# Gate and up products in a ring of three PSUM banks, and layer norms applied by ScalarE

## The chip, the cores and the metric

The kernel runs on one core of one Trainium2 chip. The metric is device time in microseconds (us) of one execution. The engines are TensorE (PE; its weight loads are PEld), VectorE (DVE), ScalarE (ACT), GpSimd (POOL) and SyncE (SP), which issues DMAs. Each runs its own instructions in program order and waits on semaphores.

## The reference

For x and a context of 16 sequences x 64 positions x 256 channels (1024 tokens), and 32 experts of width 96:

```
x = x + wkv(w, u, layernorm(x), ctx)         # keys from the norm, values from ctx
x = x + experts(layernorm(x))
layernorm(x) = (x - mean) / sqrt(var + 1e-5)
wkv, per channel, over positions t:  y = (A p + E v) / (A q + E), with decaying sums p, q
experts: softmax(x @ gate_w), the best 8 of 32, weights made to sum to 1,
  at most 64 x 8 = 512 tokens an expert (in order of tokens), then
  y = (silu(x @ w_gate[e]) * (x @ w_up[e])) @ w_down[e], weighted and summed over e
```

## The kernel before, in words

All tensors are fp32. A product of two fp32 matrices is done as three TensorE products: each operand is split into a rounded high part (made by ScalarE: whi, t_hi, h_hi, tile_hi) and the rest (wlo and t_lo by GpSimd, h_lo and tile_lo by VectorE).

**Tokens.** 1024 tokens are eight tiles of 128. The experts are computed for the first four tiles (half 0), then for the last four (half 1), for every expert with the routing weight, which is zero where an expert wasn't chosen. The first four tiles are made ready in the part before the first turn, as two units of two tiles. The other four tiles are single-tile units (slot 2): the early one partly before the first turn, the others one by one beside the expert work of half 0.

**Turns and steps.** A group is four experts, whose 384 hidden channels are three steps of 128. A turn is two groups, so six steps (k = 0 to 5); four turns (0 to 3) make a half, 24 steps. A step n on TensorE is, in order: the up product of n (six matmuls of 512 columns, `project` with part 1), when k is 0 or 3 the routing weights spread over the channels (`weights`), then small work beside it, the gate product of n+1 (`project`, part 0, six matmuls), and the down product of n-1 (`down`, six matmuls). On ScalarE a step is silu of the gate product into s_sb (L476), t_hi (L481), and a third of the next group's weights rounded, whi (L455). On VectorE: t1 = weights x silu (L977) and t = t1 x up product (L983). On GpSimd: t_lo (L348) and wlo (L323). s_sb, t1_sb and t_sb are single; t_hi, t_lo and the weights have two buffers.

**PSUM.** The gate product has two banks, 2 and 6, by the parity of k (`g_ps`), the up product one, bank 3 (`u_ps`). So the gate product of n waits for silu of n-2 (s_ready, L625) and the up product of n for t of n-1 (t_ready, L622).

**Beside half 0.** In each turn but the last a front unit (a tile) goes through its first norm at k = 0 (`stats_x`, `norm_x`), transposes and keys (`turn_kv` at k = 1, L550, `exps` at k = 2), recurrence (`recur`, at k = 3), mix and second norm (k = 4 and 5: `mix`, `turn_mixed` L559, `add_mixed`, `norm_h`); the unit before it, back, is transposed (`turn_h`, L572), split, and routed: `logits` (k = 1), `choose` (2), `ranks` (3), `weigh` (4), `turn_parts` (5, L614) and `take_route`. The lists `beside` in VectorE's and ScalarE's `turn` set after which step each stands. In turn 0 the early unit's second norm comes first.

**A norm.** VectorE makes mean and variance (`norm_stats`, L795 to L802, into mv and var), GpSimd var^-0.5 (`power`, L330), and VectorE (x - mean) x rstd, tile by tile (`norm_apply`, L807). TensorE transposes the normed tile; that is what releases `turn_kv` and `turn_h`. `keep_clock` are matmuls of zeros that fill waits before the first turn.

Of the kernel before, what the change touches and what calls it, by code (L numbers as in the profile page):

```python
# [8 lines left out]
ALU = mybir.AluOpType  # L9
# [3 lines left out]
P = 128  # L13
# [47 lines left out]
def program(nc, x, ctx_in, decay, bonus, gate_w, w_gate, w_up, w_down, out):  # L61
# [13 lines left out]
    GT = EG * INTER // P  # L75
# [14 lines left out]
    with ExitStack() as stack:  # L90
# [42 lines left out]
        var, rstd = sets("var", lambda n: [P, n]), sets("rstd", lambda n: [P, n])  # L133
        normed = sets("normed", lambda n: [P, n, C])
# [30 lines left out]
        y_ps, g_ps, u_ps, w_ps = bank[0:2], (bank[2], bank[6]), bank[3], bank[4]  # L165


# [128 lines left out]
        def _(pool):  # L296
# [67 lines left out]
            with pool.Fori(0, TURNS - 1) as it:  # L364
                turn(0, it, later(it + 3), later(it + 2))
            turn(0, TURNS - 1, None, later(TURNS + 1))
# [6 lines left out]
        def _(act):  # L373
# [22 lines left out]
            def exps(u):  # L396

                act.wait_ge(k_turned if u.slot < 2 else v_turned, u.n + 1)
                per, cols = u.tiles * BPT, u.tiles * P
                for k in range(KT):  # L400
                    fr = k_ps[u.slot][:, k * cols:(k + 1) * cols].rearrange("p (b s) -> p b s", s=S)
                    last = nc.scalar.activation(keys[u.slot][:, k * per:(k + 1) * per, 1:], fr, ACT.Exp,
                                                bias=shift[:, k:k + 1])
                last.then_inc(keys_ready, 1)

# [53 lines left out]
            for u in first_units:  # L459
                exps(u)  # L460
            act.wait_ge(gate_landed, 16)
# [6 lines left out]
            for u in first_units:  # L468
                take_h(u)
            route_exps(first_routed)  # L470

            def step(n, k, between=None):
# [3 lines left out]
                nc.scalar.activation(s_sb[:], g_ps[k % 2][:], ACT.Silu).then_inc(s_ready, 1)  # L476
# [6 lines left out]
            def turn(half, it, front, back, routed, first_turn=False, final=False):  # L483
# [45 lines left out]
        def _(pe):  # L529
# [87 lines left out]
            def project(n, half, part, slot, j, odd, group):  # L617
# [63 lines left out]
            def turn(half, it, front, back, routed, first_turn=False, last_turn=False):  # L681

                for k in range(TURN_STEPS):
                    n = it * TURN_STEPS + (half * STEPS + k)
                    slot, j = k // GT, k % GT
                    if half or not first_turn or k:
                        project(n, half, 1, slot, j, k % 2, it * 2 + (half * GROUPS + slot))
                    if back and first_turn and k == 1:

                        project(n + 1, half, 0, 0, 2, 0, 0)  # L690
# [24 lines left out]
                    elif k < TURN_STEPS - 1 or not last_turn:  # L715
                        project(n + 1, half, 0, (k + 1) // GT % 2, (k + 1) % GT, (k + 1) % 2,
                                it * 2 + (half * GROUPS + (k + 1) // GT))
                    elif half == 0:

                        pe.wait_ge(h_lo_kept, LATER)  # L720
                        project(n + 1, 1, 0, 0, 0, 0, GROUPS)
# [27 lines left out]
            project(0, 0, 0, 0, 0, 0, 0)  # L749
            project(0, 0, 1, 0, 0, 0, 0)  # L750
            ranks(first_routed)
            project(1, 0, 0, 0, 1, 1, 0)
# [16 lines left out]
        def _(dve):  # L769
# [22 lines left out]
            def norm_stats(src, *units):  # L792
# [11 lines left out]
            def norm_apply(u, src, ready, norm):  # L804
                dve.wait_ge(rstd_ready, norm + 1)
                for t in range(u.tiles):
                    last = nc.vector.tensor_scalar(normed[u.slot][:, t, :], src[:, u.tile + t, :], mv[u.slot][:, t, 0:1],  # L807
                                                   rstd[u.slot][:, t:t + 1], ALU.subtract, ALU.mult)
                last.then_inc(ready, 1)
# [4 lines left out]

            def norm_x(u):
                norm_apply(u, x_sb, k_normed, u.first_norm)
# [67 lines left out]
            def norm_h(u):  # L884
                norm_apply(u, x1, h_normed, u.second_norm)

# [63 lines left out]
            for u in first_units:  # L950
                norm_x(u)
            stats_x(early)
            recur(first_units[0])
            norm_x(early)
# [5 lines left out]
            for u in first_units:  # L960
                norm_h(u)
# [10 lines left out]
            def step(n, group):  # L972
# [10 lines left out]
                nc.vector.tensor_tensor(t_sb[:], u_ps[:], t1_sb[:], ALU.mult).then_inc(t_ready, 1)  # L983

            def turn(half, it, front, back, routed, first_turn=False):
                beside = {0: [(stats_x, front), (h_low, back), (norm_x, front)],
                          1: [(largest, routed)], 2: [(choose, routed)], 3: [(recur_and_invert, front)],
                          4: [(mix, front), (weigh, routed)], 5: [(add_mixed, front), (norm_h, front)]}
                if first_turn:
                    beside[0] = [(add_mixed, early), (norm_h, early)] + beside[0]  # L990
                for k in range(TURN_STEPS):
                    step(it * TURN_STEPS + (half * STEPS + k), it * 2 + (half * GROUPS + k // GT))
# [68 lines left out]
```

## Time and profile before

| what | value |
|---|---|
| median of 3 runs | 302.23 us (300.11 to 303.28) |
| the profiled execution: time / span | 300.93 us / 299.5 us |
| busy of the span: PE, PEld | 85%, 65% |
| busy of the span: DVE, ACT, POOL | 57%, 45%, 56% |
| granted clock of TensorE, mean | 0.924 |
| chain that ended last, by engine | PE 58%, DVE 24%, issue 11%, DMA 2%, POOL 2%, ACT 1% |

The part before the first turn ends at about 49.2 us, half 0 at about 195 us, half 1 at 294 us. A busy share is an average over these parts; a row of the table of stretches gives it for one. In a timeline row the bracket at the end is the time the engine stood idle before the instruction, and what released it. TensorE's granted clock is a share of its full 2.4 GHz; 0.50 is 1.2 GHz.

### The profile page before, as it was taken

The numbers are of one execution on the slowest core, as the hardware profiler recorded it, in microseconds if no ns is written. First come the engines' busy times: TensorE is split into PE (matmuls) and PEld (weight loads), VectorE is DVE, ScalarE is ACT, GpSimd is POOL, SyncE is SP. The second block draws the span as 40 slices with busy tenths as digits, with TensorE's granted clock in tenths as the row PEclk, the third lists the DMA queues.
The fourth block names the chain that finished last, engine by engine and source line by source line (L and its number), as shares of the span: only waits on it lengthen the run. The fifth ranks groups of instructions, "written<-read, shape, count | busy, mean of one in ns | idle before, by whom it ended". The sixth has DMA issues, their size and how long they took to land.

```text
span 299.5 us, 3887 instructions
## 1 busy us (share of the span) xinstructions
PE 255.4 (85%) x1077; PEld 194.1 (65%) x1077; DVE 169.9 (57%) x341; ACT 134.5 (45%) x211; POOL 168.3 (56%) x128
## 2 busy tenths in 40 slices
PE   5253889599399985999769997999999999999993
PEld 1222376487277764777548875787877878778772
DVE  5899956838965399544996438231533233223333
ACT  3442033293325833267334764254535635454421
POOL 5090100666445664466546776385878678786730
PEclk9956889989879995799979998899999999999999
DMA  6926000006005060140502314413250605430002
GB/s 200 291 76 158 0 2 0 0 1 165 14 0 158 0 175 2 27 131 0 158 0 64 94 46 114 102 57 87 73 146 12 160 12 146 101 126 0 0 2 71
DMA packets 39326, 22.23 MB, mean 74 GB/s; under 512 B 34192, under 2 KB 37264, under 8 KB 39312
## 3 DMA queue, kind: packets, MB, share of 16 engines
q1 hardware_dynamic: 38464, 21.63, 26.6%
q10 hardware_dynamic: 848, 0.43, 0.6%
q8 instruction: 7, 0.11, 0.2%
q14 instruction: 7, 0.06, 0.1%
HBM read 21.01 MB, written 1.05 MB: 74 GB/s over the span
## 4 chain that ended last, share of the span: by engine, by line
PE 58%; DVE 24%; issue 11%; DMA 2%; POOL 2%; ACT 1%; SPq 0%; DVEq 0%; POOLq 0%; ACTq 0%
PE bank L632 35%; PE bank L650 6%; PE bank L651 6%; PE bank L654 6%; DVE rest L943 2%; DMA x_sb<-in_x_dram 2%; DVE num L845 2%; DVE t_sb L977 2%; DVE den L845 2%; DVE state L840 2%; DVE den L856 2%; DVE state L838 1%; DVE t_sb L983 1%; DVE parts L939 1%; PE bank L639 1%
## 5 line engine op out<-in xcount | busy, mean ns | idle before, releaser
L323 POOL TENSOR_TENSOR wlo<-raw,whi 128x768 fp32r<-128x768 f32 x48 | 97.3, 2030 | 13.1 <-ACT whi L455 13.1
L348 POOL TENSOR_TENSOR t_lo<-t_sb,t_hi 128x512 fp32r<-128x512 f32 x47 | 61.0, 1297 | 72.6 <-ACT t_hi L481 72.6
L632 PE MATMUL bank<-h_hi,whi 128*128 128x512 f32 x192 | 82.9, 432 | 9.4 <-DVE t_sb L983 9.4
L977 DVE TENSOR_TENSOR t_sb<-bank,s_sb 128x512 f32<-128x512 f32 x48 | 33.2, 691 | 91.2 <-ACT s_sb L476 57.7
L481 ACT ACTIVATE t_hi<-t_sb 128x512 fp32r<-128x512 f32 x48 | 30.3, 631 | 111.1 <-DVE t_sb L983 111.1
L632 PE MATMUL bank<-h_lo,whi 128*128 128x512 f32 x192 | 79.0, 412 | 0.0
L632 PE MATMUL bank<-h_hi,wlo 128*128 128x512 f32 x192 | 78.9, 411 | 0.0
L455 ACT ACTIVATE whi<-raw 128x768 fp32r<-128x768 f32 x48 | 52.6, 1099 | 10.0 <-PE bank L654 6.7
L632 PEld LDWEIGHTS bank<-h_hi,whi 128*128 128x128 f32 x192 | 37.8, 197 | 19.1 <-DVE t_sb L983 11.2
L632 PEld LDWEIGHTS bank<-h_hi,wlo 128*128 128x128 f32 x192 | 38.0, 198 | 9.3
L632 PEld LDWEIGHTS bank<-h_lo,whi 128*128 128x128 f32 x192 | 37.9, 197 | 8.0
L650 PE MATMUL bank<-t_hi,whi 128*128 128x512 f32 x96 | 39.6, 412 | 0.1
L651 PE MATMUL bank<-t_hi,wlo 128*128 128x512 f32 x96 | 39.1, 407 | 0.0
L983 DVE TENSOR_TENSOR t_sb<-bank,t_sb 128x512 f32<-128x512 f32 x48 | 33.2, 691 | 6.2 <-PE bank L632 4.7
L654 PE MATMUL bank<-t_lo,whi 128*128 128x512 f32 x96 | 30.8, 402 | 0.0
L476 ACT ACTIVATE s_sb<-bank 128x512 f32<-128x512 f32 x48 | 28.0, 583 | 0.5 <-PE bank L632 0.4
L330 POOL TENSOR_TENSOR rstd<-var,neg_half 128x1 f32<-128x1 f32 (+1 forms) x12 | 7.3, 608 | 34.0 <-DVE var L802 34.0
L650 PEld LDWEIGHTS bank<-t_hi,whi 128*128 128x128 f32 x96 | 19.8, 206 | 4.8 <-ACT t_hi L481 0.5
L651 PEld LDWEIGHTS bank<-t_hi,wlo 128*128 128x128 f32 x96 | 19.6, 204 | 3.9
L654 PEld LDWEIGHTS bank<-t_lo,whi 128*128 128x128 f32 x96 | 19.1, 199 | 4.1
L661 PE MATMUL bank<-zeros_bf 128*128 128x512 bf16 x45 | 15.4, 506 | 5.0 <-POOL ident L307 2.6
L661 PEld LDWEIGHTS bank<-zeros_bf 128*128 128x128 bf16 x45 | 5.3, 122 | 12.7 <-issue 5.2
(113 smaller groups left out, 214.3 us busy)
## 6 DMA issues: line engine op xcount, KB each, us to landing
raw<-in_L_ffn_w_gate_dram SPq DMA_DIRECT2D x16, 384.0 KB, 3.9
raw<-in_L_ffn_w_up_dram SPq DMA_DIRECT2D x16, 384.0 KB, 4.9
raw<-in_L_ffn_w_down_dram SPq DMA_DIRECT2D x16, 384.0 KB, 5.0
out_dram<-x SPq DMA_DIRECT2D x4, 256.0 KB, 3.5
x_sb<-in_x_dram SPq DMA_DIRECT2D x1, 512.0 KB, 7.0
ctx_tile<-in_ctx_dram SPq DMA_DIRECT2D x4, 128.0 KB, 4.4
x_sb<-in_x_dram SPq DMA_DIRECT2D x1, 256.0 KB, 3.2
ctx_sb<-in_ctx_dram SPq DMA_DIRECT2D x1, 256.0 KB, 4.7
```

The lines of the kernel that those rows point to most:

```text
L323: pool.tensor_tensor(split_view(wlo, slot, part), raw_parts(slot, part), split_view(whi, slot, part).bitcast(F32), ALU.subtract).then_inc( ...
L348: pool.tensor_tensor(t_lo[k % 2][:], t_sb[:], t_hi[k % 2][:].bitcast(F32), ALU.subtract).then_inc(t_lo_ready, 1)
L455: nc.scalar.activation(split_view(whi, slot, part), raw_parts(slot, part), ACT.Copy).then_inc(w_hi_ready, 1)
L476: nc.scalar.activation(s_sb[:], g_ps[k % 2][:], ACT.Silu).then_inc(s_ready, 1)
L481: nc.scalar.activation(t_hi[k % 2][:], t_sb[:], ACT.Copy).then_inc(t_hi_ready, 1)
L632: last = nc.tensor.matmul(ps[:], up_weight(w, slot, part, k, j), h[:, k, tokens], start=(i == 0), stop=(i == len(terms) - 1))
L650: nc.tensor.matmul(y_ps[m][:], down_weight(whi, slot, j, m), t_hi[odd][:], start=False, stop=False)
L651: nc.tensor.matmul(y_ps[m][:], down_weight(wlo, slot, j, m), t_hi[odd][:], start=False, stop=False)
L654: last = nc.tensor.matmul(y_ps[m][:], down_weight(whi, slot, j, m), t_lo[odd][:], start=False, stop=last_step)
L661: nc.tensor.matmul(bank[7][:], zeros_bf[:, 0:P], zeros_bf[:], start=(i == 0), stop=(i == count - 1))
L977: nc.vector.tensor_tensor(t1_sb[:], w_ps[:], s_sb[:], ALU.mult).then_inc(t1_ready, 1)
L983: nc.vector.tensor_tensor(t_sb[:], u_ps[:], t1_sb[:], ALU.mult).then_inc(t_ready, 1)
```

## The change

Two things. **The ring**: gate and up products take banks 2, 3 and 6 in turn, gate of step k the bank 2k mod 3, up the bank 2k+1 mod 3. So the gate product of n now waits for t of n-2 and the up product of n for silu of n-1. **The norms**: VectorE also makes the negated mean, GpSimd multiplies it with rstd to offset (a wait on its own chain between the two), and ScalarE applies rstd x + offset as one activation with a scale and a bias operand. GpSimd's `power` and VectorE's `norm_stats` get waits that keep the single buffers of slot 2 from being overwritten.

```diff
+        ring = (bank[2], bank[3], bank[6])
+
+        def g_ps(k):
+            return ring[2 * k % 3]
+
+        def u_ps(k):
+            return ring[(2 * k + 1) % 3]
...
                 pool.wait_ge(var_ready, norm + 1)
-                pool.tensor_tensor(rstd[u.slot][:], var[u.slot][:], neg_half[:, 0:u.tiles], ALU.pow).then_inc(rstd_ready, 1)
+                if u.slot == 2 and u is not early:
+
+                    if norm is u.first_norm:
+                        pool.wait_ge(h_normed, u.n)
+                    else:
+                        pool.wait_ge(k_normed, u.n + 1)
+                chain.link(pool.tensor_tensor(rstd[u.slot][:], var[u.slot][:], neg_half[:, 0:u.tiles], ALU.pow))
+                pool.tensor_tensor(offset[u.slot][:], neg_mean[u.slot][:], rstd[u.slot][:], ALU.mult).then_inc(rstd_ready, 1)
...
+            def norm_apply(u, src, ready, norm):
+
+                act.wait_ge(rstd_ready, norm + 1)
+                for t in range(u.tiles):
+                    tile = u.tile + t
+                    last = nc.scalar.activation(normed[u.slot][:, t, :], src[:, bass.ds(tile, 1), :] if u.slot == 2 else src[:, tile, :],
+                                                ACT.Identity, bias=offset[u.slot][:, t:t + 1], scale=rstd[u.slot][:, t:t + 1])
+                last.then_inc(ready, 1)
...
             for u in first_units:
+                norm_x(u)
+            for u in first_units:
                 exps(u)
+            norm_x(early)
...
             spread_experts()
             for u in first_units:
+                norm_h(u)
+            for u in first_units:
                 take_h(u)
...
-                    beside[0] = lambda: take_route(first_routed)
+                    beside[0] = lambda: (take_route(first_routed), norm_h(early))
...
                         split_high(ahead % 2, k % GT, it * 2 + (half * GROUPS + ahead))
+                    if front and k == (1 if first_turn else 0):
+                        norm_x(front)
+                    if front and k == TURN_STEPS - 1:
+                        norm_h(front)
                     if back and k == TURN_STEPS - 1:
                         take_route(routed)
...
-                ps, ready = ((g_ps[odd], g_ready), (u_ps, u_ready))[part]
-                if part == 1:
-                    pe.wait_ge(t_ready, n + 1)
-                elif not isinstance(n, int) or n >= 2:
-
-                    pe.wait_ge(s_ready, n - 1)
+
+
+                ps, ready = ((g_ps(j), g_ready), (u_ps(j), u_ready))[part]
+                if part == 0 and (not isinstance(n, int) or n >= 2):
+                    pe.wait_ge(t_ready, n)
+                elif part == 1 and (not isinstance(n, int) or n >= 1):
+                    pe.wait_ge(s_ready, n)
...
                 for u in units:
+                    if src is x_sb and u.slot == 2 and u is not early:
+                        dve.wait_ge(rstd_ready, u.first_norm)
+                    nc.vector.tensor_scalar(neg_mean[u.slot][:], mv[u.slot][:, :, 0], -1.0, None, ALU.mult)
                     nc.vector.tensor_scalar(var[u.slot][:], mv[u.slot][:, :, 1], EPS, None, ALU.add).then_inc(var_ready, 1)
...
-                beside = {0: [(stats_x, front), (h_low, back), (norm_x, front)],
+                beside = {0: [(stats_x, front), (h_low, back)],
                           1: [(largest, routed)], 2: [(choose, routed)], 3: [(recur_and_invert, front)],
-                          4: [(mix, front), (weigh, routed)], 5: [(add_mixed, front), (norm_h, front)]}
+                          4: [(mix, front), (weigh, routed)], 5: [(add_mixed, front)]}
                 if first_turn:
-                    beside[0] = [(add_mixed, early), (norm_h, early)] + beside[0]
+                    beside[0] = [(add_mixed, early)] + beside[0]
```

ScalarE in turn 0, steps 0 to 2, before (L476 silu, L442 the routing weights copied, L481 t_hi, L455 whi, L426 and L428 the back tile's high part):

```order
L476 ACTIVATE s_sb<-bank 128x512
L442 ACTIVATE route<-bank 96x512
L481 ACTIVATE t_hi<-t_sb 128x512
L455 ACTIVATE whi<-raw 128x768
L476 ACTIVATE s_sb<-bank 128x512
L426 ACTIVATE tile_hi<-bank 128x256
L428 ACTIVATE h_hi<-tile_hi 128x2x128
L481 ACTIVATE t_hi<-t_sb 128x512
L455 ACTIVATE whi<-raw 128x768
L476 ACTIVATE s_sb<-bank 128x512
```

The same after the change (its own line numbers: L514 silu, L475 route, L519 t_hi, L488 whi, L459 and L461 the high part, L428 the norms):

```order
L514 ACTIVATE s_sb<-bank 128x512
L475 ACTIVATE route<-bank 96x512
L428 ACTIVATE normed<-x,offset,rstd 128x256
L519 ACTIVATE t_hi<-t_sb 128x512
L488 ACTIVATE whi<-raw 128x768
L514 ACTIVATE s_sb<-bank 128x512
L459 ACTIVATE tile_hi<-bank 128x256
L461 ACTIVATE h_hi<-tile_hi 128x2x128
L519 ACTIVATE t_hi<-t_sb 128x512
L488 ACTIVATE whi<-raw 128x768
L428 ACTIVATE normed<-x_sb,offset,rstd 128x256
L514 ACTIVATE s_sb<-bank 128x512
```

The early unit's second norm now stands between silu and t_hi of step 0, and the front unit's first norm between whi of step 1 and silu of step 2. In turns 1 and 2 the front unit's first norm stands between whi of step 0 and silu of step 1, and its second norm behind whi of step 5.

VectorE before the first turn, from the second norm's variances to h_lo, before:

```order
L802 TENSOR_SCALAR var<-mv 128x2 x2
L835 TENSOR_SCALAR values<-bank 128x4
L836 TENSOR_TENSOR values<-keys,bank 128x4x64
L838 SCALAR_TENSOR_TENSOR state<-factors,keys 128x260
L840 SCALAR_TENSOR_TENSOR state<-factors,values 128x260
L845 SCALAR_TENSOR_TENSOR den<-keys,gain,state 128x128 x2
L845 SCALAR_TENSOR_TENSOR num<-values,gain,state 128x128 x2
L807 TENSOR_SCALAR normed<-x,mv,rstd 128x256 x4
L963 TENSOR_TENSOR gate_lo<-gate_sb,gate_hi 128x64
L856 RECIPROCAL den<-den 128x256
L892 TENSOR_TENSOR h_lo<-bank,h_hi 128x2x256 x2
```

After the change the four rows of L807 are gone there, and each var has a neg_mean ahead of it; the rest stands in the same order.

## Rows read from the trace of the kernel before

**Rows 1.** table of stretches: length, busy us by engine, granted clock, DMA share, GB/s
```profile
84.10:120.10 36.00, 31.22 (x128) 24.19 (x127) 25.30 (x48) 17.44 (x28) 21.07 (x15) 0.88 0.26 70
219.20:294.00 74.80, 74.54 (x319) 59.27 (x318) 25.01 (x37) 35.37 (x51) 51.52 (x32) 1.00 0.26 71
```

**Rows 2.** what TensorE waited for: us in total, times, longest
```profile
PE bank L550 <- DVE normed L807: 10.0, 5, 5.3
PE bank L632 <- DVE t_sb L983: 9.4, 3, 3.2
PE bank L614 <- DVE parts L945: 6.5, 4, 2.1
```

**Rows 3.** timeline of TensorE, turn 1, step 5: start, us, engine, line
```profile
114.40 0.80 PE L632 MATMUL bank<-h_hi,whi 128*128 128x512 f32 x1 [3.11 <-DVE t_sb L983]
...
118.92 0.34 PE L614 MATMUL bank<-ident_bf,parts 128*96 128x128 bf16 x1 [1.17 <-DVE parts L945]
```

**Rows 4.** timeline of VectorE, turn 1, steps 3 to 5
```profile
104.20 0.69 DVE L977 TENSOR_TENSOR t_sb<-bank,s_sb 128x512 f32<-128x512 f32 x1 [2.54 <-PE bank L639]
...
112.93 0.69 DVE L977 TENSOR_TENSOR t_sb<-bank,s_sb 128x512 f32<-128x512 f32 x1
...
118.68 0.19 DVE L945 TENSOR_TENSOR parts<-rest,parts 128x32 bf16<-128x32 f32 x1
```

**Rows 5.** timeline before the first turn, VectorE and GpSimd
```profile
32.37 0.24 DVE L802 TENSOR_SCALAR var<-mv 128x2 f32<-128x2 f32 x2
...
35.15 1.37 DVE L807 TENSOR_SCALAR normed<-x,mv,rstd 128x256 f32<-128x256 f32 x4
...
38.36 1.29 DVE L892 TENSOR_TENSOR h_lo<-bank,h_hi 128x512 fp32r<-128x512 f32 x2
...
32.62 1.48 POOL L330 TENSOR_TENSOR rstd<-var,neg_half 128x2 f32<-128x2 f32 x2 [9.89 <-DVE var L802]
```

**Rows 6.** timeline of turn 0, steps 0 and 1, four engines
```profile
52.33 0.56 POOL L330 TENSOR_TENSOR rstd<-var,neg_half 128x1 f32<-128x1 f32 x1 [18.23 <-DVE var L802]
...
50.84 0.63 ACT L481 ACTIVATE t_hi<-t_sb 128x512 fp32r<-128x512 f32 x1 [1.93 <-DVE t_sb L983]
...
52.51 0.58 ACT L476 ACTIVATE s_sb<-bank 128x512 f32<-128x512 f32 x1
...
54.88 0.38 ACT L426 ACTIVATE tile_hi<-bank 128x256 fp32r<-128x256 f32 x1 [1.79 <-PE bank L572]
...
57.81 0.68 DVE L977 TENSOR_TENSOR t_sb<-bank,s_sb 128x512 f32<-128x512 f32 x1
...
57.95 0.51 PE L550 MATMUL bank<-ident,normed 128*128 128x128 f32 x2 [3.10 <-DVE normed L807]
...
59.25 0.63 ACT L481 ACTIVATE t_hi<-t_sb 128x512 fp32r<-128x512 f32 x1 [3.53 <-DVE t_sb L983]
...
60.94 0.58 ACT L476 ACTIVATE s_sb<-bank 128x512 f32<-128x512 f32 x1
```

**Rows 7.** groups by line and shape: count, busy us, mean ns of one, idle before
```profile
L402 ACT ACTIVATE keys<-bank,shift 128x256 f32<-128x256 f32 x4 | 1.7, 469 | 1.0 <-PE bank L550 0.9
L330 POOL TENSOR_TENSOR rstd<-var,neg_half 128x1 f32<-128x1 f32 x8 | 4.4, 545 | 22.3 <-DVE var L802 22.3
```

**Rows 8.** timeline of turn 1, steps 0 and 1, three engines
```profile
86.75 1.92 DVE L807 TENSOR_SCALAR normed<-x,mv,rstd 128x256 f32<-128x256 f32 x1 [1.13 <-POOL rstd L330]
...
89.44 0.69 DVE L977 TENSOR_TENSOR t_sb<-bank,s_sb 128x512 f32<-128x512 f32 x1 [0.76 <-PE bank L639]
...
94.25 0.58 ACT L476 ACTIVATE s_sb<-bank 128x512 f32<-128x512 f32 x1
...
94.16 0.48 PE L550 MATMUL bank<-ident,normed 128*128 128x128 f32 x2 [0.50 <-DVE normed L807]
```

**Rows 9.** table of stretches at the end of turns 1 and 2
```profile
119.10:123.60 4.50, 4.50 (x12) 3.53 (x12) 2.99 (x7) 2.21 (x5) 2.66 (x3) 0.50 0.00 0
155.70:156.50 0.80, 0.77 (x4) 0.62 (x5) 0.77 (x2) 0.00 (x0) 0.00 (x0) 1.00 0.00 0
```

More of the change, by code:

```diff
@@ L133, in program @@
         var, rstd = sets("var", lambda n: [P, n]), sets("rstd", lambda n: [P, n])
+        neg_mean, offset = sets("neg_mean", lambda n: [P, n]), sets("offset", lambda n: [P, n])
         normed = sets("normed", lambda n: [P, n, C])
@@ L164, in program @@
         bank = [stack.enter_context(nc.psum_tensor(f"bank{i}", [P, 512], F32)) for i in range(8)]
-        y_ps, g_ps, u_ps, w_ps = bank[0:2], (bank[2], bank[6]), bank[3], bank[4]
+        y_ps, w_ps = bank[0:2], bank[4]
+        ring = (bank[2], bank[3], bank[6])
[3 more added lines that the diff above has]
+            return ring[(2 * k + 1) % 3]
         k_ps = [bank[0], bank[2], bank[5]]
@@ L364, in _ @@
             with pool.Fori(0, TURNS - 1) as it:
+                chain.enter(it, 2)
                 turn(0, it, later(it + 3), later(it + 2))
+            chain.leave(TURNS - 1)
             turn(0, TURNS - 1, None, later(TURNS + 1))
@@ L404, in exps, with norm_x, norm_h @@
                 last.then_inc(keys_ready, 1)
+            def norm_apply(u, src, ready, norm):
[5 more added lines that the diff above has]
+                last.then_inc(ready, 1)
+            def norm_x(u):
+                act.wait_ge(x_landed[u.slot], 32 if u.slot == 0 else 16)
+                norm_apply(u, x_sb, k_normed, u.first_norm)
+            def norm_h(u):
+                norm_apply(u, x1, h_normed, u.second_norm)
             def invert():
@@ L475, in step @@
                 act.wait_ge(t1_ready, n + 1)
-                nc.scalar.activation(s_sb[:], g_ps[k % 2][:], ACT.Silu).then_inc(s_ready, 1)
+                nc.scalar.activation(s_sb[:], g_ps(k)[:], ACT.Silu).then_inc(s_ready, 1)
                 if between:
@@ L615, in turn_parts, with project @@
                 last.then_inc(parts_turned, 1)
-            def project(n, half, part, slot, j, odd, group):
+            def project(n, half, part, slot, j, group):
                 tokens = slice(half * HALF, (half + 1) * HALF)
-                ps, ready = ((g_ps[odd], g_ready), (u_ps, u_ready))[part]
-                if part == 1:
-                    pe.wait_ge(t_ready, n + 1)
-                elif not isinstance(n, int) or n >= 2:
-                    pe.wait_ge(s_ready, n - 1)
+                ps, ready = ((g_ps(j), g_ready), (u_ps(j), u_ready))[part]
[3 more added lines that the diff above has]
+                    pe.wait_ge(s_ready, n)
                 if j == 0:
@@ L686, in turn @@
                     if half or not first_turn or k:
-                        project(n, half, 1, slot, j, k % 2, it * 2 + (half * GROUPS + slot))
+                        project(n, half, 1, slot, j, it * 2 + (half * GROUPS + slot))
                     if back and first_turn and k == 1:
-                        project(n + 1, half, 0, 0, 2, 0, 0)
+                        project(n + 1, half, 0, 0, 2, 0)
                         turn_h(back)
@@ L715, in turn @@
                     elif k < TURN_STEPS - 1 or not last_turn:
-                        project(n + 1, half, 0, (k + 1) // GT % 2, (k + 1) % GT, (k + 1) % 2,
+                        project(n + 1, half, 0, (k + 1) // GT % 2, (k + 1) % GT,
                                 it * 2 + (half * GROUPS + (k + 1) // GT))
@@ L801, in norm_stats @@
                 for u in units:
+                    if src is x_sb and u.slot == 2 and u is not early:
+                        dve.wait_ge(rstd_ready, u.first_norm)
+                    nc.vector.tensor_scalar(neg_mean[u.slot][:], mv[u.slot][:, :, 0], -1.0, None, ALU.mult)
                     nc.vector.tensor_scalar(var[u.slot][:], mv[u.slot][:, :, 1], EPS, None, ALU.add).then_inc(var_ready, 1)
[L804 to L809, printed above, removed]
             def stats_x(u):
@@ L949, in _ @@
             bonus_parts()
-            for u in first_units:
-                norm_x(u)
             stats_x(early)
             recur(first_units[0])
-            norm_x(early)
             recur(first_units[1])
@@ L970, in _, with step @@
             weigh(first_routed)
-            def step(n, group):
+            def step(n, k, group):
                 dve.wait_ge(w_turned, group + 1)
```

18 lines of the change are left out of this document (6 added, 12 removed).

## The prediction

> **What bounds the kernel now.** I read four views. First the table of stretches [rows 1]. In the second half of the tokens (the second row) TensorE is busy 74.54 of 74.80 us at the full granted clock: that stretch is the matmuls and nothing else. A turn of the first half has the same six steps plus small transposes and routing matmuls, but the turn from 84.10 to 120.10 takes 36.0 us against some 25.2 us for six steps of the second half (74.80 us hold about 17.8 steps of 4.2 us), and TensorE's clock is 0.88 there. What can be won lies in the first half and in the part before it.
>
> Second, what TensorE waits for [rows 2]: normalized tiles (L550, 10.0 us, most of it before the first turn and in turn 0), t_sb for the up product (L632, 9.4 us in three waits), and the routing parts (L614, 6.5 us in four). The 9.4 us are what the ring is about: the up product of step k+1 writes the only up bank, which VectorE's product of step k reads.
>
> Third, the place of such a wait [rows 3]. In turn 1 the up product of step 5 starts at 114.40 after 3.11 us of idle, and 1.17 us more go by until the routing parts are transposed at 118.92. The gate product that follows starts behind that transpose, in program order.
>
> Fourth, VectorE at the same place [rows 4]: step 3's product starts at 104.20, released by TensorE's weights matmul; then the recurrence fills VectorE until 112.93, where step 4's product starts, and the parts are done at 118.68+0.19 = 118.87. None of these instructions reads anything of the up product of step 5. So **the wait for t_sb lies inside a longer wait for the parts**.
>
> **The change, term by term,** in us on the path that sets the end.
>
> *Ring.* The up product no longer waits for the last t but for the silu of the step before (long done: ScalarE runs it while VectorE is in the recurrence); the gate product now waits for the t of two steps back, done long before. In turn 1 the up product starts about 3.1 us earlier, ends by about 112.6, and TensorE then stands until VectorE's mixed tile and parts arrive at 118.9, as before. The three waits of 9.4 us thus become longer waits on L559 and L614. Gain in time: 0. Ends: -9.4 if the parts were not what binds, 0 by the rows. In the second half no wait on t_sb is there to remove: 0.
>
> *Before the first turn.* VectorE loses four normalizations of 256 elements right before the reciprocal and h_lo (1.37 us from 35.15 on), and gains two neg_mean, which I take as 0.16 together, since the two var took 0.24 [rows 5]: net -1.2. ScalarE makes them instead: GpSimd's two power end at 32.62+1.48 = 34.1, with two neg_mean ahead and two multiplications between them about 35.0, its two tiles are ready at 35.9, transposed by 36.6, copied by 37.4, and h_lo of the first pair can start when VectorE is free, at 38.36-1.2 = 37.2. So VectorE is still last, and the router's first matmul moves by -1.2. The early unit's normalization also leaves VectorE between the two recurrences (0.3 us, of which I count 0.1, because VectorE's scans there run beside GpSimd's subtractions and seem to end with them). The first two norms move behind ScalarE's exponentials of the decay, but the first recurrence waits longer, for the early tile's statistics ahead of it on VectorE: 0. Sum: **-1.3** (ends -1.6 and -0.5; a further -1.5 if the clock then stays up in the first products).
>
> *Turn 0.* Here the order is bad for ScalarE's queue. Before [rows 6]: t_hi of step 0 runs at 50.84, silu of step 1 at 52.51, and both normalizations are VectorE's; TensorE transposes the front tile at 57.95. Now the normalization of the early unit stands in ScalarE's queue between silu and t_hi of step 0, and it needs rstd: power starts at 52.33+0.08, takes 0.56, the new multiplication lies between 0 and a power's 0.545 [rows 7]; I take 0.35 with its wait: 53.3. ScalarE's normalization is not in the trace; the nearest row is the exp with a bias operand, 0.469 [rows 7]: done at 53.85. Then t_hi, the weight copy and silu of step 1 take what they took, 50.84 to 53.09 = 2.25: 56.1. Behind them tile_hi (0.38), VectorE's h_lo (0.4, as wide, ahead of step 1's products on its queue), the two products (57.81 to 59.25 = 1.44 to the start of t_hi): 58.4. Then t_hi and the weight copy, 59.25 to 60.94 = 1.69: 60.1, and only there norm_x of the front tile, 0.47: TensorE transposes at 60.55 instead of 57.95. Behind that transpose TensorE does 18 matmuls of step 2 and so on without waiting until weights of step 3, which release VectorE's chain as in [rows 4]; nothing absorbs it. **+2.6** (ends +1.3, if the multiplication is free and the copies shrink, and +3.3).
>
> The Trainium skill (ScalarE: Activation LUTs, What ACT_TABLE_LOAD costs) states 186 ns plus 0.833 ns an element and about 93 ns for each per-partition pointer operand: by it, as an estimate, the two-operand normalization of 256 elements takes 0.585 us where I take 0.469 from the row, and the sum would be 0.4 larger. No row of before shows an activation with both operands.
>
> *Turns 1 and 2.* norm_x of the front tile now stands between the weight copy and silu of step 1. Before, silu started at 94.25 and the transposes at 94.16, after 0.50 of idle [rows 8]. Now the norm runs 94.25 to 94.72, the transposes start at 94.78: +0.6 each, on the path since TensorE has no other wait until step 5. **+1.2** for two turns (ends 0.6 and 2.4). GpSimd's rstd is there before ScalarE is free. The other norm, at step 5, is off VectorE, where it started at 86.75, behind rstd. ScalarE does it from 86.75+0.35 = 87.1 to 87.6, the route copy, the table's touch and silu of step 0 (some 1.0 together) follow until 88.6, and VectorE waits for the weights matmul until 89.44 as before: 0, covered by 0.8 us. Without that cover each turn would pay what it lacks. GpSimd's extra multiplication pushes a weight subtraction by 0.35 into idle time behind it: 0. The new waits of power for h_normed and k_normed are on things done in the steps before: 0. Steps of turn 3 have no front tile: 0.
>
> *Clock.* TensorE's granted clock falls in these waits and comes back later: 0.50 from 119.10 to 123.60 in turn 1, but already 1.00 from 155.70 in turn 2 [rows 9], where the up product at half clock had just been run inside the wait. 4.5 us at half clock cost about half of themselves, some 2. With the ring the up product moves ahead of the wait and the idle time is in one piece of about 6.3 us. I take that turn 2 then pays most of what turn 1 pays: **+1.2** (ends -2 and +2.5; the first if it returns everywhere as in turn 2).
>
> Sum: -1.3 + 2.6 + 1.2 + 1.2 = **+3.7** on the profiled execution's 300.93 (span 299.5 and 1.4 around it), 304.6. That execution lies 1.3 below the median of the runs shown, inside their spread; I go half of it up and say **305.2**.
>
> **Rivals.** *The ring pays.* If VectorE's blocked small instructions before the parts shrink (with other phases beside GpSimd), the parts come first and the 9.4 us are won: with the rest of the sum 300.93 + 3.7 - 9.4 - 1.2 (no idle, no clock term) = 294.0. For it: the waits are real; and the normalization that goes took 1.92 us [rows 8] against 0.34 each of the four in [rows 5], which ran with GpSimd idle. Against: what blocks in steps 3 to 5 is not what is removed. Faster if more than 6.7 of the 9.4 come through. The Trainium skill (SBUF — State Buffer, on the shared port pair) says that a VectorE instruction in a two-port mode and a GpSimd one block each other fully: the 1.92 us row agrees, and by that rule each normalization beside GpSimd gives VectorE back up to 1.9 us, which is 7 us over four norm_h: the case above, not my sum, if that time were on the path. Chance 0.13.
>
> *Nothing measurable.* The delay in turn 0 is nearer its lower end and the clock term is nil or a gain: -1.3 + 1.3 + 0.6 to 1.2 + 0 gives 301.5 to 302.1 on the profile, about 302.5 in runs. For it: ScalarE idles in most steps and may absorb more than I see. Chance 0.24.
>
> *ScalarE becomes the late one at each turn's start.* norm_h waits for GpSimd, and silu of step 0 stands behind it; if it comes over 0.8 us later than I reckon, VectorE's first product is late in turns 1 to 3 and with it the parts and silu of step 1. At 1.5 us a turn: 304.6 + 4.5 = 309.1. Chance 0.10.
>
> **Forecast:** the sum, 302.5 to 307.5, chance 0.53. About 1% is what a measurement of this kernel can tell from no change (299.2 to 305.3); my number sits on that line, so the forecast gives 0.33 to slower and 0.20 to the same. Together: faster 0.13, within 1% 0.44, slower 0.43. The range 299.5 to 309.0 leaves out the first rival and the upper part of the last.
>
> **What would show it.** The wait on L632 for t_sb is gone and L559 and L614 have grown by about 9 us: the ring step is right; if the turn from weights of step 3 to the parts is shorter than 14.7 us, it is wrong. In turn 0 the front tile's transposes start some 1.3 us later than 57.95 (2.6 less the 1.3 won before). In turns 1 and 2 TensorE idles about 1.1 us before them. An ACTIVATE of normed takes about 0.47 us, with no extra table load. A granted clock of 1.00 right after the parts in all turns would take 1.2 and more off the sum; a silu of step 0 that ends later than weights would add.

## The result and the profile after

The changed kernel took 307.92 us (median of 4 runs with before's 302.04 beside it), ratio 1.0188, interval 1.0129 to 1.0247. Six more runs in the experiments gave 308.19 against 301.73, ratio 1.0223 (1.018 to 1.0267). It is **slower by about 2%**, 6 us.

One of the four executions, and the only one profiled with them, took 835.13 us; the profile below is of the repeated kernel, 308 us like the other three. The ratio 1.0188 leaves the 835 out as a slow run and takes in a fifth execution of 306.80. What was odd in the 835 us is told at the end.

What TensorE waited for, after (the columns of [rows 2]):

```profile
PE bank L656 <- DVE parts L978: 13.3, 4, 3.7
PE bank L601 <- DVE mixed L906: 12.7, 5, 5.1
PE bank L592 <- ACT normed L428: 11.1, 5, 6.0
```

The three waits for t_sb (9.4 us) are gone. The waits for parts and mixed were 6.5 and 5.5 and are 26.0 together: 14 more, not less. The waits for normalized tiles (now ScalarE's) went from 10.0 to 11.1.

TensorE's transposes of the routing parts close the last step of each turn of half 0, and the transposes of y_sb (L678, after L721) come at the end of the half. The timeline rows of before that [rows 3] doesn't show:

```profile
47.89 0.28 PE L614 MATMUL bank<-ident_bf,parts 128*96 128x128 bf16 x2
...
82.91 0.34 PE L614 MATMUL bank<-ident_bf,parts 128*96 128x128 bf16 x1 [2.10 <-DVE parts L945]
...
155.73 0.26 PE L614 MATMUL bank<-ident_bf,parts 128*96 128x128 bf16 x1 [1.16 <-DVE parts L945]
...
184.90 0.26 PE L614 MATMUL bank<-ident_bf,parts 128*96 128x128 bf16 x1 [2.07 <-DVE parts L945]
...
193.97 0.71 PE L678 MATMUL bank<-ident,y_sb 128*128 128x128 f32 x5
```

and those of after:

```profile
46.62 0.38 PE L656 MATMUL bank<-ident_bf,parts 128*96 128x128 bf16 x4
...
85.26 0.34 PE L656 MATMUL bank<-ident_bf,parts 128*96 128x128 bf16 x1 [3.71 <-DVE parts L978]
...
123.87 0.34 PE L656 MATMUL bank<-ident_bf,parts 128*96 128x128 bf16 x1 [3.70 <-DVE parts L978]
...
162.12 0.34 PE L656 MATMUL bank<-ident_bf,parts 128*96 128x128 bf16 x1 [3.71 <-DVE parts L978]
...
193.69 0.26 PE L656 MATMUL bank<-ident_bf,parts 128*96 128x128 bf16 x1 [2.17 <-DVE parts L978]
...
202.69 0.49 PE L721 MATMUL bank<-ident,y_sb 128*128 128x128 f32 x3
```

The differences are the budget. Beside it, from tables of 0.5 us stretches, TensorE's idle time and its busy time at half clock (before > after):

| from to | before | after | change | idle | busy at half clock |
|---|---|---|---|---|---|
| start to first parts | 47.89 | 46.62 | -1.3 | 18.5 > 17.6 | 12.0 > 11.2 |
| turn 0 | 35.02 | 38.64 | +3.6 | 9.1 > 12.5 | 4.7 > 6.5 |
| turn 1 | 36.01 | 38.61 | +2.6 | 4.8 > 7.4 | 6.9 > 7.6 |
| turn 2 | 36.81 | 38.25 | +1.4 | 4.8 > 7.3 | 8.1 > 6.4 |
| turn 3 | 29.17 | 31.57 | +2.4 | 2.1 > 2.1 | 0.0 > 5.6 |
| to y_sb | 9.07 | 9.00 | -0.1 | 0.1 > 0.1 | 3.4 > 3.4 |
| rest of the span | 105.53 | 104.21 | -1.3 | 4.7 > 4.7 | 0.0 > 0.0 |

The sum is +7.4, the difference of the spans (306.9 - 299.5). Two rows of it are surprises: turn 3, where the idle time is the same and the clock is what differs, and the second half, 1.3 us shorter where the change has nothing to do.

In turns 0 to 2 part of the half clock of before lies in the up product that runs inside the wait for the parts, where it costs nothing. So here is the part of each turn that sets its length: from the parts to the routing weights of step 3 in turns 0 to 2, and the whole of turn 3. From those weights to the next parts both kernels take 15.1 to 15.2 us in each turn. Before (the columns of [rows 1]):

```profile
47.89:67.75 19.86, 15.89 (x70) 11.52 (x68) 10.80 (x24) 11.23 (x18) 10.02 (x9) 0.91 0.00 0
82.91:103.77 20.86, 20.36 (x87) 16.18 (x87) 10.93 (x26) 12.59 (x22) 12.01 (x10) 0.92 0.21 57
118.92:140.53 21.61, 21.11 (x87) 16.67 (x87) 10.92 (x26) 12.58 (x22) 11.98 (x10) 0.88 0.21 55
155.73:184.90 29.17, 27.10 (x122) 21.52 (x122) 16.73 (x34) 16.79 (x26) 20.36 (x14) 1.00 0.31 82
```

and after:

```profile
46.62:70.12 23.50, 16.81 (x70) 12.76 (x68) 8.32 (x24) 12.16 (x20) 10.77 (x11) 0.78 0.00 1
85.26:108.71 23.45, 22.02 (x87) 17.43 (x87) 9.67 (x26) 13.94 (x24) 13.92 (x13) 0.84 0.19 51
123.87:146.96 23.09, 21.67 (x87) 17.15 (x87) 8.72 (x26) 13.91 (x24) 13.70 (x13) 0.86 0.19 51
162.12:193.69 31.57, 29.40 (x122) 23.37 (x122) 14.96 (x34) 17.40 (x27) 20.49 (x15) 0.91 0.28 76
```

The same numbers of matmuls keep TensorE busy 0.9, 1.7, 0.6 and 2.3 us longer, 5.4 in all, at a lower granted clock; its idle time is 2.7, 0.9, 0.9 and 0.1 us longer, 4.7 in all.

Turn 0 on four engines, steps 0 and 1 (the rows of [rows 6]):

```profile
51.10 0.56 POOL L344 TENSOR_TENSOR rstd<-var,neg_half 128x1 f32<-128x1 f32 x1 [16.05 <-DVE var L848]
51.74 0.19 POOL L345 TENSOR_TENSOR offset<-neg_mean,rstd 128x1 f32<-128x1 f32 x1
...
51.96 0.60 ACT L428 ACTIVATE normed<-x,offset,rstd 128x256 f32<-128x256 f32 x1 [4.33 <-POOL offset L345]
52.47 0.61 ACT L519 ACTIVATE t_hi<-t_sb 128x512 fp32r<-128x512 f32 x1
...
56.77 0.63 ACT L519 ACTIVATE t_hi<-t_sb 128x512 fp32r<-128x512 f32 x1 [1.36 <-DVE t_sb L1011]
...
58.43 0.59 ACT L428 ACTIVATE normed<-x_sb,offset,rstd 128x256 f32<-128x256 f32 x1
...
59.07 0.70 PE L592 MATMUL bank<-ident,normed 128*128 128x128 f32 x2 [5.95 <-ACT normed L428]
```

t_hi of step 0 waits behind the norm, the front tile's norm stands behind the weight copy of step 1, and TensorE idles 5.95 us where it idled 3.10. The norm takes 0.59 to 0.60, the multiplication 0.19.

Turn 1: the wait before the front tile's transposes, and then four stretches: behind the parts, at those transposes, from 1.7 us after their start on, and at the start of turn 3:

```profile
97.64 0.48 PE L592 MATMUL bank<-ident,normed 128*128 128x128 f32 x2 [1.43 <-ACT normed L428]
```

```profile
85.26:89.00 3.74, 3.74 (x10) 2.97 (x11) 2.40 (x7) 1.37 (x2) 1.72 (x2) 0.50 0.01 2
97.60:99.00 1.40, 1.36 (x11) 1.39 (x12) 0.99 (x2) 0.28 (x1) 1.40 (x1) 1.00 0.00 0
99.30:102.90 3.60, 3.60 (x10) 2.81 (x9) 0.88 (x3) 3.46 (x4) 2.93 (x3) 0.54 0.00 0
162.40:168.00 5.60, 5.60 (x15) 4.40 (x15) 2.12 (x7) 2.70 (x6) 3.76 (x4) 0.51 0.00 0
```

The wait grew from 0.50 [rows 8] to 1.43, and behind it there is **a fall of the clock that before didn't have**: ten matmuls in 3.6 us where before 17 ran in 3.5 at 1.00. The last row is the start of turn 3 at half clock, where before had 1.00 from 155.70 on [rows 9]. The two stretches of before, 1.8 us after the start of the like transposes, and at the start of turn 3:

```profile
96.00:99.50 3.50, 3.50 (x17) 2.87 (x16) 1.12 (x3) 3.11 (x4) 3.33 (x4) 1.00 0.00 0
155.73:158.00 2.27, 2.27 (x10) 1.87 (x11) 2.00 (x4) 0.96 (x2) 0.25 (x1) 1.00 0.00 0
```

### The profile page after: what moved, and what is told of

It is laid out like the page before. It is cut to its first block, busy times and chain, and to the rows that moved or that the text cites. A ratio compares the mean times of both kernels' runs of the same rounds, so it can differ in the third digit from the quotient of the medians.

```text
span 833.7 us, 3934 instructions
## 1 busy us (share of the span) xinstructions
PE 816.6 (98%) x1077; PEld 424.2 (51%) x1077; DVE 156.9 (19%) x337; ACT 146.2 (18%) x227; POOL 168.6 (20%) x140
## 4 chain that ended last, share of the span: by engine, by line
PE 96%; DVE 2%; ACT 0%; issue 0%; POOL 0%; DVEq 0%; POOLq 0%; ACTq 0%
PE bank L675 57%; PE bank L697 10%; PE bank L694 9%; PE bank L693 9%; PE bank L704 4%; PE bank L632 2%; PE bank L682 2%; PE bank L592 1%; PE bank L614 1%; PE bank L721 1%; PE bank L601 1%; DVE state L876 0%; DVE state L874 0%; PE bank L708 0%; DVE den L881 0%
## 5 line engine op out<-in xcount | busy, mean ns | idle before, releaser
L675 PE MATMUL bank<-h_hi,whi 128*128 128x512 f32 x192 | 219.9, 1145 | 0.0
L675 PE MATMUL bank<-h_hi,wlo 128*128 128x512 f32 x192 | 209.0, 1089 | 0.0
L675 PE MATMUL bank<-h_lo,whi 128*128 128x512 f32 x192 | 209.0, 1089 | 0.0
L675 PEld LDWEIGHTS bank<-h_lo,whi 128*128 128x128 f32 x192 | 85.2, 444 | 69.0 <-issue 69.0
L675 PEld LDWEIGHTS bank<-h_hi,wlo 128*128 128x128 f32 x192 | 81.6, 425 | 71.1 <-issue 70.4
L675 PEld LDWEIGHTS bank<-h_hi,whi 128*128 128x128 f32 x192 | 82.8, 431 | 66.6 <-issue 65.9
L694 PE MATMUL bank<-t_hi,wlo 128*128 128x512 f32 x96 | 104.9, 1093 | 0.0
L693 PE MATMUL bank<-t_hi,whi 128*128 128x512 f32 x96 | 103.9, 1082 | 0.0
L519 ACT ACTIVATE t_hi<-t_sb 128x512 fp32r<-128x512 f32 x48 | 30.3, 630 | 386.2 <-DVE t_sb L1011 386.2
L697 PE MATMUL bank<-t_lo,whi 128*128 128x512 f32 x96 | 92.5, 1107 | 0.0
L488 ACT ACTIVATE whi<-raw 128x768 fp32r<-128x768 f32 x48 | 52.3, 1093 | 77.8 <-PE bank L697 77.8
L514 ACT ACTIVATE s_sb<-bank 128x512 f32<-128x512 f32 x48 | 28.5, 595 | 89.7 <-PE bank L675 89.7
L704 PE MATMUL bank<-zeros_bf 128*128 128x512 bf16 x45 | 37.9, 1092 | 5.5 <-ACT inv L444 2.9
```

Source lines behind the costliest of these rows:

```text
L488: nc.scalar.activation(split_view(whi, slot, part), raw_parts(slot, part), ACT.Copy).then_inc(w_hi_ready, 1)
L514: nc.scalar.activation(s_sb[:], g_ps(k)[:], ACT.Silu).then_inc(s_ready, 1)
L519: nc.scalar.activation(t_hi[k % 2][:], t_sb[:], ACT.Copy).then_inc(t_hi_ready, 1)
L675: last = nc.tensor.matmul(ps[:], up_weight(w, slot, part, k, j), h[:, k, tokens], start=(i == 0), stop=(i == len(terms) - 1))
L693: nc.tensor.matmul(y_ps[m][:], down_weight(whi, slot, j, m), t_hi[odd][:], start=False, stop=False)
L694: nc.tensor.matmul(y_ps[m][:], down_weight(wlo, slot, j, m), t_hi[odd][:], start=False, stop=False)
```

## Experiments

Each ratio is to before, run on the same chip in the same rounds. The four kernels from the tensors alone to the late parts with the ring ran on another chip than the other eight; before's median was 301.74 us there, and 301.73 and 302.53 beside the others. Turns and stretches are read from one trace of each kernel.

**The changed kernel again** (no edit).

> The changed kernel once more, for a trace at the usual matmul pace. My theory (ScalarE's queue delays the front tile's transposes in turn 0, a little in turns 1 and 2, the clock takes some more, the ring gives nothing): ratio to before 1.012 to 1.025; the front tile's transposes of turn 0 about 1.3 us later than 57.95; TensorE idles about 1.1 us before them in turns 1 and 2; waits for t_sb gone, waits for mixed and parts grown by about 9 us. Rival (ScalarE is the late one at every turn's start): silu of step 0 ends after the weights matmul in turns 1 to 3, and the time lost is spread over the turns.

Measured: 308.19 us, 1.0223 (1.018 to 1.0267). Transposes of turn 0 at 59.07, 1.1 later; TensorE idles 1.43 and 1.42 us before those of turns 1 and 2, where 1.1 was expected. The rival (ScalarE late at a turn's start) is out: VectorE's first product of turn 1 was released by TensorE's weights, 1.3 us after silu's end at 90.71 (0.9 us in turn 2, 1.9 in turn 3):

```profile
92.02 0.69 DVE L1005 TENSOR_TENSOR t_sb<-bank,s_sb 128x512 f32<-128x512 f32 x1 [3.98 <-PE bank L682]
```

**The ring alone.** Before, with the diff's ring, `project` and bank arguments, the norms left as they were.

> Before, with the ring of three banks alone; the norms stay VectorE's. Theory that the ring gives nothing and costs clock: ratio 1.000 to 1.006 (0 for the three waits of 9.4 us, which turn into waits for mixed and parts, and up to 1.8 us of clock). Rival, the ring pays: 0.97 (9 us less).

Measured: 304.91 us, **1.0112** (1.0072 to 1.0152): the ring does not give nothing, it costs about 3 us, more than the 1.006 expected at most. Between the parts' transposes the turns take 35.6, 35.8, 36.7 and 31.8 us; against before that is +0.6, -0.2, -0.1 and +2.6. Turn 3 has the cost, and there it is the clock (table of stretches):

```profile
156.90:162.10 5.20, 5.20 (x13) 4.12 (x13) 3.70 (x7) 2.21 (x5) 3.47 (x3) 0.50 0.00 0
```

**The norms alone.** The changed kernel with the banks and waits of before (of the edit, the banks; `project` gets the two waits of before back):

```diff
         def g_ps(k):
-            return ring[2 * k % 3]
+            return (bank[2], bank[6])[k % 2]
         def u_ps(k):
-            return ring[(2 * k + 1) % 3]
+            return bank[3]
...
```

> The changed kernel with the gate and up banks and waits of before; the norms are ScalarE's. Theory: the loss lies in the norms, so ratio 1.010 to 1.020, as the changed kernel less up to 1.8 us of clock. Rival (ring and norms cost about alike, or the loss needs both): under 1.008.

Measured: 306.16 us, **1.0156** (1.0113 to 1.0198). The larger part, as forecast: turn 0 takes 38.2, turn 1 38.4. Turn 3 takes 30.3, with 3.1 us at half clock: a late clock at the start of turn 3 doesn't need the ring.

**The first units' norms alone.** `norm_apply` of slots 0 and 1 on ScalarE, slot 2 as before.

> Before, with ScalarE's norms for the first two units alone, both norms of each; single-tile units keep VectorE's. Theory: the part before the first turn becomes 1.2 us shorter and nothing else changes, ratio 0.996 (0.994 to 0.999). Rival (the norm's chain over GpSimd's multiplication and ScalarE is as long as VectorE's): 1.000 or above.

Measured: 299.78 us, **0.9932** (0.9901 to 0.9964): faster, and by more than the part before the first turn explains (first parts 0.8 us earlier). Its second half is as short as the changed kernel's. That led to the next kernel.

**Tensors alone.**

```diff
+        neg_mean, offset = sets("neg_mean", lambda n: [P, n]), sets("offset", lambda n: [P, n])
         normed = sets("normed", lambda n: [P, n, C])
```

> Before, with the six small tensors neg_mean and offset allocated and never used, so that everything allocated after them in SBUF lies a few bytes further, as in the kernels with ScalarE's norms. Theory (the second half's products run at 0.227 to 0.230 us apart instead of 0.233 because of where their operands lie): the second half 1.3 us shorter, the first about 1 us, ratio 0.992 to 0.996. Rival (the norms themselves do it): 1.000.

Measured: 300.69 us, **0.9947** (0.9914 to 0.9979). Not one instruction is added. The second half from the transposes of y_sb to those at its end, before:

```profile
193.97:294.45 100.48, 99.77 (x433) 79.61 (x431) 34.60 (x54) 48.64 (x70) 71.01 (x44) 1.00 0.26 71
```

and with the unused tensors:

```profile
195.37:294.58 99.21, 98.45 (x431) 79.64 (x431) 34.63 (x54) 48.59 (x70) 70.93 (x44) 1.00 0.26 72
```

1.27 us less for the same work at the same clock. The products with h_lo and h_hi come 0.227 to 0.228 us apart instead of 0.232 to 0.234, those with t_hi 0.233 instead of 0.231 to 0.233. From the transposes of y_sb to those at the end all eight traces of kernels with these tensors take 99.2 us, and all five without take 100.5. So what moves when six small tensors are allocated ahead, that is, where later tensors lie in SBUF, changes the pace of the h products by 2 to 3%. Which tensor's place does it wasn't tried. Every kernel that has these tensors starts from about 0.9947, the norms cost more than their ratios say, and what the first units' norms give by themselves can't be told from nothing in the times: 0.9932 (0.9901 to 0.9964) against 0.9947.

**The ring's banks with the old wait.** The up product again waits for the last t (the edit is shown against the ring alone):

```diff
-                elif part == 1 and (not isinstance(n, int) or n >= 1):
-                    pe.wait_ge(s_ready, n)
+                elif part == 1:
+                    pe.wait_ge(t_ready, n + 1)
```

> The ring of three banks, but the up product still waits for the last t, as before. Theory (the ring costs because the up product of step 5 runs early, so that TensorE then stands in one piece and comes back at half clock): ratio 0.998 to 1.003, and turn 3 begins at full clock. Rival (the banks or the gate product's new wait cost): 1.008 to 1.012 as the ring alone.

Measured: 302.23 us, **1.0001** (0.9977 to 1.0025). So the ring's cost comes with the up product's early start; its banks and the gate product's new wait cost nothing that shows. Turn 3 begins at full clock:

```profile
156.90:160.00 3.10, 3.10 (x14) 2.51 (x15) 2.32 (x6) 1.80 (x5) 1.09 (x1) 1.00 0.00 0
```

**Routing parts later on TensorE**, first without the ring, then with it. The edit in TensorE's `turn`:

```diff
-                    if back and k == 5:
-                        turn_parts(routed)
                     if half == 0 and first_turn and k == 0:
...
                     if back and k == 0 and not first_turn:
                         turn_h(back)
+                    if back and k == 5:
+                        turn_parts(routed)
```

> Before, with the transposes of the routing parts moved on TensorE from behind the up product of step 5 to behind that step's gate and down products. Theory (the parts set the end of the wait in each turn of half 0): 2 to 3 us less in each of turns 0 to 2 and about 2 in turn 3, ratio 0.965 to 0.985. Rival (VectorE's product of step 5 sets the end anyway): 0.995 to 1.000.

Measured: 297.13 us, **0.9851** (0.9816 to 0.9886). Weights to weights, turn 0's 39.9 us become 38.4 and turn 1's 36.8 become 35.3. The wait on parts did hold TensorE, but by 1.5 us in these two turns and not the 2 to 3 expected; turn 2 becomes no shorter (34.6 and 35.0).

> The same move with the ring of three banks (norms as before). Theory (the ring was hidden behind the parts, and now the up product no longer waits for t): about 1 us a turn less than the move alone, ratio 0.955 to 0.980 and 0.003 to 0.012 under the move alone. Rival (the ring gains nothing anywhere, and costs clock): at or above the move alone.

Measured: 299.93 us, **0.993** (0.9891 to 0.9968): the theory falls. Even with the parts out of the way the ring makes it slower, by 0.8%. Turn 1 has the largest loss. From weights to weights, without the ring:

```profile
86.14:121.42 35.28, 29.77 (x128) 23.20 (x128) 25.38 (x47) 17.26 (x29) 21.04 (x16) 0.95 0.26 71
```

with it:

```profile
85.86:124.24 38.38, 32.66 (x128) 25.46 (x128) 26.66 (x48) 17.76 (x30) 21.21 (x16) 0.87 0.24 65
```

The same 128 matmuls, as much idle time (5.5 and 5.7), and 2.9 us more of busy time at the lower mean clock. TensorE still waits for VectorE's mixed tile behind the up product (2.11 us, released at 117.78). The half clock is not at that place alone: with the ring the wait before the front tile's transposes is 2.57 us instead of 1.59, and from 93.8 to 100.6 the clock is 0.5, where without the ring it stays at 1.00. The other turns differ in both directions: with the ring turn 0 takes 36.6 instead of 38.4, turn 2 34.8 instead of 35.0, and turn 3, to the transposes of y_sb, 33.9 instead of 32.9. So in this trace the ring gains 1.7 us in turn 0 and loses more than that in turns 1 and 3.

**The front tile's norm ahead of the weight copy.** In ScalarE's `turn`:

```diff
-                    beside[1] = lambda: take_h(back)
+                    beside[1] = lambda: (take_h(back), norm_x(front))
...
                     if back and k == 0 and not first_turn:
                         take_h(back)
+                        if front:
+                            norm_x(front)
...
-                    if front and k == (1 if first_turn else 0):
-                        norm_x(front)
```

> The changed kernel with the front tile's first norm one place further ahead in ScalarE's queue: right behind the back tile's high part (turn 0: within step 1, ahead of t_hi; turns 1 and 2: ahead of the weight copy of step 0). Theory (the norm stands behind a weight copy, and the wait of 1.43 us before its transposes brings the half clock after it): TensorE's wait before them falls to about 3 us in turn 0 and 0.8 in turns 1 and 2, the granted clock stays 1.00 after them in turns 1 and 2, ratio to before 1.003 to 1.012, that is 3 to 6 us under the changed kernel. Rival (the chain through GpSimd's two instructions sets the norm, not its place): 1.018 to 1.022.

Measured, ring and norms as in the change: 302.41 us, **0.9995** (0.9967 to 1.0022). One norm moved ahead brings the time back to that of before, which is better than the 1.003 to 1.012 expected; against the unused tensors alone (0.9947) about 0.5% is still lost. TensorE waits 2.93 us before the transposes of turn 0 and 1.06 in turn 1:

```profile
56.16 0.50 PE L592 MATMUL bank<-ident,normed 128*128 128x128 f32 x2 [2.93 <-ACT normed L428]
...
94.94 0.47 PE L592 MATMUL bank<-ident,normed 128*128 128x128 f32 x2 [1.06 <-ACT normed L428]
```

and the clock stays up behind the second:

```profile
94.94:96.40 1.46, 1.46 (x12) 1.41 (x13) 0.00 (x0) 1.38 (x2) 0.39 (x1) 1.00 0.00 0
96.40:99.90 3.50, 3.50 (x17) 2.88 (x16) 1.48 (x3) 2.04 (x3) 3.34 (x4) 1.00 0.00 0
```

17 matmuls in 3.5 us there, against 10 in 3.6 in the changed kernel.

> The same place for the norm, without the ring. Theory: ratio 0.993 to 1.002, since before the first turn 1 us is won, the operands lie better (0.995 by themselves) and half 0 loses little. Rival as above: 1.010 to 1.016.

Measured: 302.71 us, 1.001 (0.9981 to 1.004), inside what was expected. Without the ring it is no faster than with it. So the ring's 1.1% alone is not a price that can be added to others: in this company it costs nothing. In both profiles turn 3 takes 31.0 to 31.1 us, with 4.5 to 4.6 us at half clock, ring or not. So beside ScalarE's norms the late clock of turn 3 can't be put down to the ring alone.

> ScalarE's norms for the first two units alone, and the routing parts transposed behind the gate and down products of step 5; no ring. If the two gains add: 0.993 x 0.985 = 0.978 (0.974 to 0.982). If the clock takes one of them back: 0.984 to 0.988.

Measured: **294.93 us, 0.9735** (0.9693 to 0.9778), the fastest kernel here, faster than before and than the change. The gains add (0.978 was their product), and whether they give more than that is inside the noise. Turn 3 takes 27.5 us without any half clock, as it does with the late parts alone (28.0).

> All norms ScalarE's, in the earlier place, with the late parts and without the ring. If ScalarE's single-tile norms cost nothing in the better place: 0.975 to 0.985, as the first units' norms with late parts. If they still cost: 0.986 or more.

Measured: 297.32 us, 0.9823 (0.9776 to 0.987). Inside the first range, but 0.9% above the kernel whose single-tile norms stayed on VectorE: ScalarE's still cost there. Its trace has 40.1 us in turn 1, with 10.2 us at half clock, where the other kernel's has 35.1 and 3.3.

## Why the prediction was right, and where it was not

**Direction and range: right; the size of the loss: about half.** 305.2 was said, 299.5 to 309.0, and 307.9 measured, 2.7 us off. The forecast's own band ended at 307.5, just below. The sum was +3.7 on a profiled span that grew by 7.4. In its parts, from the rows of the stretches: before the first turn -1.3 (forecast -1.3), idle time +4.7 (forecast 2.6 + 1.2 = 3.8), busy time for the same matmuls **+5.4 (forecast 1.2, for the clock)**, the second half -1.3 (not forecast). So the clock was the step that was mis-sized, by more than its upper end of 2.5, and that the time still fell into the range is partly luck: the unforeseen gain of the second half took some of it back, and the range was wide. One reading of the prediction is a little off, with nothing hanging on it: a step of the second half is 4.27 us (the weights of a group come every 12.8), so six steps are 25.6 us and not 25.2. By step:

- *Ring, no gain on the path.* Right: with the old wait kept the kernel takes what before takes, with the early start it takes more. The waits for t_sb became waits for mixed and parts, and weights to parts still takes what [rows 4] shows, 14.7 us (109.14 to 123.82 in turn 1). I expected the two waits to grow by 9; they grew by 14. The rest is the up product itself: in three turns it ran inside the gap, up to 2.7 us long, and now runs ahead of it, 1.4 long.
- *Before the first turn, -1.3.* Right, with the mechanism. VectorE comes to h_lo straight from the reciprocal, and from the means and variances to h_lo it takes 5.2 us instead of 6.4. First parts at 46.62 for 47.89: -1.27. That this agrees to the tenth is luck, since single traces differ there: 46.7 to 48.9 in the six kernels whose part before the first turn is the old one, 46.0 to 47.7 in the seven with ScalarE's norms there; the means differ by 1.1.

```profile
31.96 0.38 DVE L799 BATCH_NORM_AGGREGATE mv<-stats 128x2 f32<-128x6 f32 x4 [0.15 <-DVE stats L795]
```

```profile
31.85 0.38 DVE L842 BATCH_NORM_AGGREGATE mv<-stats 128x2 f32<-128x6 f32 x4 [0.15 <-DVE stats L838]
...
35.31 1.74 DVE L892 RECIPROCAL den<-den 128x256 f32<-128x256 f32 x1
37.09 1.29 DVE L925 TENSOR_TENSOR h_lo<-bank,h_hi 128x512 fp32r<-128x512 f32 x2
```

- *Turn 0, +2.6.* Against the first parts the front tile's transposes moved by 12.45 - 10.06 = +2.4. The turn itself grew by 3.6; the rest is mostly 0.9 of busy time, but the kernels with the unused tensors and with the ring's banks and the old wait, where nothing else changed, show 0.7 and 0.9 more there too, so it can be the scatter of single traces. The parts of the sum were off in opposite ways: multiplication and its wait 0.27 for 0.35, norm 0.59 for 0.47. Here the Trainium skill (ScalarE: Activation LUTs, What ACT_TABLE_LOAD costs) was the better guide: the estimate of 0.585 us by its figures is what the trace shows, 0.59.
- *Turns 1 and 2, +0.6 each.* **Under-sized, and the mechanism half seen.** The wait grew by 0.9, and a clock fall came behind it that cost about 1.6 in turn 1. I had looked for the clock only at the end of a turn. Moving the norm ahead shortened the wait to 1.06 and 1.10, and the fall was gone: the norm's late place brings both. The length of the wait doesn't decide by itself: with the late parts TensorE waits 1.59 and 1.57 us there and no fall follows, and in the fastest kernel one of two waits of 1.59 is followed by one.
- *Clock, +1.2.* Right in kind, wrong in size and place. I expected turn 2's end to lose the full clock; it did, and that is the +2.4 of turn 3 in the budget, 5.6 us at half clock. The ring alone measured +3.2 us, over my upper end of 2.5. The clock's part comes from the norms as well as from the ring. In the same stretches of a turn, against before, in us:

| kernel | idle | busy, same matmuls |
|---|---|---|
| ring alone | +0.2 | +2.9 |
| norms alone | +4.6 | +2.5 |
| the change | +4.7 | +5.4 |
| the change, front tile's norm earlier | +1.0 | +3.2 |

- *Not in the sum at all:* the six small tensors move what lies behind them, -0.5% (about -1.6 us). Without this the change would have been some 8 us slower, as an estimate from that ratio.

Of the rivals, the ring that pays would have needed parts that come first; the late parts took that obstacle away, and the ring still didn't pay: it gained in turn 0 and lost more in the others. Nothing measurable is what the change is with the norm in the better place. What stays open is why the clock comes back after 3 us in one turn and after 5 in the next: the runs show how much is lost, and that it moves with the ring and with the norm's place, not a rule to foretell it in a turn.

## What to carry to other kernels

Before a wait is removed, follow what is queued behind it on the waiting engine: if a longer wait ends later anyway, the work only moves ahead and the idle time becomes one piece, after which TensorE may run at half clock for microseconds, as here. When an operation moves to another engine's queue, its place among the copies there can matter more than its own length: one norm a turn, 0.59 us long, put ahead of a weight copy was worth 2% here. Put what TensorE waits for ahead of what it doesn't. And test a change against a kernel that only allocates the same tensors.

## What the runs showed of the hardware that was not expected

- Six small unused tensors, allocated ahead of the matrix operands, made the 431 matmuls of the second half 1.27 us shorter in all, at the same granted clock.
- One execution of the changed kernel took 835.13 us. Its trace (lines by group, as in [rows 7]) has a granted clock of 1.00 and matmuls of 512 columns that take 1.1 us, where the repeated kernel's average at both clocks is near 0.4; weight loads take 0.43 us for 0.20. The largest groups of VectorE, ScalarE and GpSimd took their usual times.

```profile
L675 PE MATMUL bank<-h_hi,whi 128*128 128x512 f32 x192 | 219.9, 1145 | 0.0
...
L675 PE MATMUL bank<-h_lo,whi 128*128 128x512 f32 x192 | 209.0, 1089 | 0.0
...
L519 ACT ACTIVATE t_hi<-t_sb 128x512 fp32r<-128x512 f32 x48 | 30.3, 630 | 386.2 <-DVE t_sb L1011 386.2
```

It came once in eleven executions of this kernel and in none of another; no run here tells its cause.
